# Moving one quantisation block out of the first attention, and the first feed-forward stage's start into that attention's last turn

## The reference

```python
# layer 0: attention with 32 heads of 128 (8 key/value heads), then a 4-bit linear layer
x = x + tanh(g_xattn[0]) * L0_xattn(layernorm(x), ctx, wq, wk, wv, wo)
w_fp = ((nibbles(W_q) - zero) * scale).reshape(512, 512)
x = x + tanh(g_ffn[0]) * layernorm(x) @ w_fp.T
# layer 1: attention with 32 heads of 16, then a linear layer with 28 gated low-rank experts
x = x + tanh(g_xattn[1]) * L1_xattn(rmsnorm(layernorm(x)) * ln_w, ctx)
logits = xf @ gate_W.T;  top_vals, top_idx = top_k(logits, 2);  gate = softmax(top_vals)
x = x + tanh(g_ffn[1]) * (xf @ base_W.T + lora(xf, gate))
# layer 2: attention with one head of width 512, then a SiLU layer with NF4 weights
x = x + tanh(g_xattn[2]) * softmax(Q @ K.T / sqrt(512)) @ features
normalized = w / absmax(block of 64)
dq = NF4_CODE[searchsorted(bounds, normalized)] * absmax        # for w1, w2 and w3
x = x + tanh(g_ffn[2]) * (silu(x @ dq1.T) * (x @ dq2.T)) @ dq3.T
# layer 3: attention with 32 heads of 128, then stream mixing with a Sinkhorn iteration
```

## Time and profile before

| what | value |
|---|---|
| median of three runs | 1779.58 us |
| profiled execution, its own time | 1778.58 us |
| its span in the trace | 1776.9 us |
| PE busy | 1436.3 us (81%) |
| DVE busy | 1172.7 us (66%) |
| ACT busy | 607.6 us (34%) |
| POOL busy | 357.5 us (20%) |
| TensorE clock granted in the profiled execution | 0.896 of full speed |

### The profile page before, as it was taken

One profiled execution on the slowest core, in us unless ns is written; L12 is line 12 of the kernel. 1 busy time (PEld: TensorE's weight loads), 2 busy tenths in 40 slices (PEclk: granted clock), 3 DMA queues, 4 the chain that ended last, 5 costly groups with the idle time before them and its releaser, 6 DMA issues.

```text
span 1776.9 us, 18410 instructions
## 1 busy us (share of the span) xinstructions
PE 1436.3 (81%) x6556; PEld 1012.6 (57%) x6556; DVE 1172.7 (66%) x1816; ACT 607.6 (34%) x912; POOL 357.5 (20%) x404
## 2 busy tenths in 40 slices
PE   7999999995386885888788888799999999995104
PEld 5665665552164554656466666567777777774101
DVE  4899999989746884323544445566665666576778
ACT  3655555554212332111222111344444344442003
POOL 1222222222244002001201111121122122214500
PEclk9999999998687996895699999899999999997556
DMA  4799999998710000020101121010011011000001
GB/s 185 192 217 225 219 209 219 215 194 167 176 47 11 1 1 24 1 71 1 36 18 38 45 86 48 12 60 24 36 60 60 25 36 60 1 1 1 0 0 48
DMA packets 40128, 136.35 MB, mean 77 GB/s; under 512 B 5184, under 2 KB 11200, under 8 KB 33840
## 3 DMA queue, kind: packets, MB, share of 16 engines
q0 software_dynamic: 13824, 51.91, 15.8%
q1 hardware_dynamic: 26224, 83.38, 14.1%
HBM read 72.63 MB, written 10.75 MB: 47 GB/s over the span
## 4 chain that ended last, share of the span: by engine, by line
PE 49%; DVE 20%; DMA 11%; issue 11%; DVEq 4%; ACT 3%; POOL 1%; POOLq 1%; SPq 0%
DMA AR<-AR 11%; PE PS L151 10%; PE PS L153 9%; PE PS L152 9%; DVE AR L626 4%; PE PS L841 4%; PE PS L877 3%; DVE AR L2118 2%; DVE AR L2112 2%; DVE AR L2116 2%; PE PS L863 2%; DVE X L1854 1%; PE PS L255 1%; PE PS L1982 1%; DVE AR L632 1%
## 5 line engine op out<-in xcount | busy, mean ns | idle before, releaser
L412 POOL DMA_DIRECT2D AR<-AR x96 | 97.5, 1054 | 349.0 <-DMA AR<-AR 146.3
L508 PE MATMUL PS<-R,PT 128*128 128x512 f32 x256 | 127.9, 646 | 44.1 <-DVE X L660 44.1
L153 PE MATMUL PS<-R16r 128*128 128x512 f32 (+1 forms) x312 | 123.3, 395 | 0.0
L152 PE MATMUL PS<-R16r 128*128 128x512 f32 (+1 forms) x328 | 122.6, 374 | 0.0
L483 PE MATMUL PS<-R,HT 128*128 128x256 f32 x512 | 115.9, 379 | 0.0
L508 PEld LDWEIGHTS PS<-R,PT 128*128 128x128 f32 x256 | 50.9, 206 | 108.1 <-issue 107.2
L483 PEld LDWEIGHTS PS<-R,HT 128*128 128x128 f32 x512 | 94.8, 190 | 11.6
L151 PE MATMUL PS<-R16r,HTr 128*128 128x512 f32 (+1 forms) x224 | 92.3, 412 | 6.1 <-DVE X L1234 4.6
L151 PE MATMUL PS<-HTr,R16r 128*128 128x512 f32 (+1 forms) x240 | 89.5, 373 | 3.1 <-DVE R16r L193 1.6
L152 PE MATMUL PS<-R16r,HTr 128*128 128x512 f32 (+1 forms) x224 | 87.6, 391 | 0.0
L153 PE MATMUL PS<-HTr,R16r 128*128 128x512 f32 (+1 forms) x240 | 87.2, 363 | 0.0
(11 more groups left out here) (285 smaller groups left out, 3627.9 us busy)
## 6 DMA issues: line engine op xcount, KB each, us to landing
AR<-AR POOLq DMA_DIRECT2D x96, 528.0 KB, 6.1
OR<-in_wo SPq DMA_DIRECT2D x12, 1024.0 KB, 7.7
dequantised<-AR SPq DMA_DIRECT2D x8, 1056.0 KB, 6.4
WR<-in_w0q SPq DMA_DIRECT2D x8, 1024.0 KB, 9.6
AR<-in_w3q SPq DMA_DIRECT2D x8, 1024.0 KB, 4.8
WR<-dequantised SPq DMA_DIRECT2D x22, 256.0 KB, 2.7
AR<-in_nf SPq DMA_DIRECT2D x4, 1056.0 KB, 8.0
nf_in<-in_nf SPq DMA_DIRECT2D x4, 1056.0 KB, 6.5
```

Of the source, the lines that this page charges most:

```text
L152: nc.tensor.matmul(out, ah, bl, start=False, stop=False)
L153: return nc.tensor.matmul(out, al, bh, start=False, stop=last_)
L412: nc.gpsimd.dma_start(nf_below(g)[:, part], what[:, part], accum_op=ALU.add, max_dma_last_dim=4 * N_NF // 2).then_inc(added, 16)
L508: i = nc.tensor.matmul(bank(5 + tt), PT[:, at:at + P], vo[:, pr, b, :], start=pr == 0, stop=pr == 1)
```

## The change

1. Quantisation of block 7 (`LATE`) leaves x0. Its maxima, scaling and first two `down` masks go to f1, between the norm and the wait for the logits. Ups 0 and 1 and `lowest` come after the expert weights, ups 2 to 5 and downs 2 and 3 stand between f1's sums, and ups 6 and 7 and downs 4 and 5 at the head of a2. ACT's ramps stand in f1. POOL's accumulations stand before, in and behind `pool_norm(pool, 4)`, and the join is behind the scaling of f2's first two blocks. SP stores the block after f2's first two loads, and f2's other loads wait for that store. The masks with even numbers use space in `R16`.
2. The last four turns of x0 have DVE's unpacking one turn earlier, and hold f0's low part (now on DVE) and the norm of tiles 0 to 3 with their `low` for two. PE turns tiles 0 and 1 before the last `outputs`.
3. a1's key projection runs on PE after `outputs(30)`; the value projection stays in f0, behind its third product. PE runs f0 as one product behind each tile.
4. DVE's sums of f0 are mixed with the norm's remaining steps (`dve_f0`).

```diff
...
+        def pe_norm(pe, n, work=None, given=0):
+            for t in range(given, T + 2):
+                if t < T:
+                    pe_norm_tile(pe, n, t)
+                else:
                     pe.wait_ge(lo_ready, T * (n - 1) + t - 1)
...
         def nf_mask(g, k):
+            if g == LATE and k % 2 == 0:
+                return R16[:, 4096:4096 + N_NF]
             return nf_ring(g + 1 if k % 2 else g + 2)
...
+        def nf_store(sp, g):
...
+            if g == LATE - 1:
+                sp.dma_start(KR_W, l1kr_d).then_inc(A1["kr_in"], 16)
...
+                if u == NU0 - 1:
+                    pe.wait_ge(A0["piece_sb"], PIECES0 * NG)
+                    pe_norm_tile(pe, 1, 0)
+                    pe_norm_tile(pe, 1, 1)
                 outputs(u)
+                if u == NU0 - 2:
+                    pe_a1_keys(pe)
...
-                far(g, 2 * b + 1)
+                if g < LATE:
+                    far(act, g, 2 * b + 1)
                 if u + 2 < NU0:
                     exps(u + 2)
-                far(g, 2 * b + 2)
+                if g < LATE:
+                    far(act, g, 2 * b + 2)
...
+                if u == NU0 - 2:
+                    act.wait_ge(F0["packed"], 1)
+                    act.wait_ge(A0["s_mm"], NU0)
+                    nc.scalar.copy(Oh[:], OR[:]).then_inc(F0["w_hi"], 1)
...
-            for u in range(NU0):
+            for u in range(LATE * B):
                 g, b = divmod(u, B)
-                more = g + 1 < NG
...
+                if b:
+                    dve_stats(dve, b - 1)
                 if u + 1 < NU0:
                     norm(u + 1)
-                if b == 0:
-                    down(g, 1)
-                    down(g, 0)
-                else:
-                    if b == 2:
-                        down(g, 4)
-                    up(g, 2 * b - 1)
-                    if b == 1:
-                        down(g, 2)
-                if more and b == 2:
-                    nf_reciprocal(g + 1)
                 if u + 2 < NU0:
                     shift(u + 2)
-                if 0 < b < 3:
-                    down(g, 2 * b + 1)
-                if more and b == 0:
-                    nf_max(g + 1)
-                up(g, 2 * b)
                 if b == 0:
-                    lowest(g)
-                if b == 3:
-                    up(g, 7)
-                    dve.drain().then_inc(A0["nf_used"], 1)
-                if more and b == 3:
-                    nf_normalise(g + 1)
-                if g == NG - 1 and b == 1:
                     dve_f0_nibbles(dve)
-                if g == NG - 1 and b == 2:
+                elif b == 1:
                     dve_f0_scale(dve)
+                elif b == 2:
+                    dve_f0_low(dve)
+                    norm_scaled(dve, 1, 0)
+                    norm_scaled(dve, 1, 1)
+                else:
+                    norm_scaled(dve, 1, 2)
+                    norm_low(dve, 1, 0)
+                    norm_scaled(dve, 1, 3)
+                    norm_low(dve, 1, 1)
             add(NU0 - 1)
+            dve_stats(dve, PAIRS - 1)
...
-        F0_BANKS = (5, 7, 3)
+        F0_BANKS = (7, 5, 6)
         def pe_f0(pe):
             def product(t):
                 if t == 0:
                     pe.wait_ge(F0["split"], 1)
+                if t == 1:
                     pe.wait_ge(A0["acc"], 2 * NU0)
                 if t >= 3:
                     pe.wait_ge(F0["acc"], t - 2)
...
-                if t == 1:
-                    pe_a1_keys(pe)
-            pe.wait_ge(A0["piece_sb"], PIECES0 * NG)
-            pe_norm(pe, 1, lambda t: product(t) if t < 3 else None)
-            for t in range(3, T):
-                product(t)
+                if t == 2:
+                    pe_a1_values(pe)
+            pe_norm(pe, 1, product, 2)
...
+        def dve_f0_low(dve):
+            dve.wait_ge(F0["w_hi"], 1)
+            nc.vector.tensor_tensor(Ol[:], OR[:], Oh[:].bitcast(F32), ALU.subtract).then_inc(F0["split"], 1)
...
+        def dve_f0(dve):
+            for t in range(4, T):
+                norm_low(dve, 1, t - 2)
+                norm_scaled(dve, 1, t)
+                sum_tile(dve, F0, 0, 1, F0_BANKS, t - 4)
+            norm_low(dve, 1, T - 2)
+            norm_low(dve, 1, T - 1)
+            for t in range(4, T):
+                sum_tile(dve, F0, 0, 1, F0_BANKS, t)
...
         def pool_a1(pool):
-            pool.wait_ge(A0["nf_stored"], 16 * NG)
+            pool.wait_ge(A0["nf_stored"], 16 * LATE)
...
             pe.wait_ge(A1["kr_in"], 16)
+            pe.wait_ge(A0["shifted"], NU0)
...
+            i.then_inc(A1["kr_mm"], 1)
+        def pe_a1_values(pe):
             pe.wait_ge(A1["w_in"], 16)
+            pe.wait_ge(A0["pt_ready"], NU0)
...
+        def act_a1_keys(act):
             act.wait_ge(A1["kr_mm"], 1)
...
+        def act_a1(act):
+            act.wait_ge(A1["kr_mm"], 2)
...
+            far(act, LATE, 1)
+            far(act, LATE, 2)
...
+                if t + 3 <= NUP:
+                    far(act, LATE, t + 3)
         def dve_f1(dve):
             dve_norm(dve, 3, PAIRS - 1)
+            nf_max(dve, LATE)
+            nf_reciprocal(dve, LATE)
+            nf_normalise(dve, LATE)
+            dve.drain()
+            down(dve, LATE, 1)
+            down(dve, LATE, 0)
             dve.wait_ge(F1["lg_ready"], T)
...
-            dve_sum(dve, F1, 1, 1, (2, 3, 4, 5))
+            up(dve, LATE, 0)
+            lowest(dve, LATE)
+            up(dve, LATE, 1)
+            for t in range(T):
+                sum_tile(dve, F1, 1, 1, (2, 3, 4, 5), t)
+                if t == 0:
+                    up(dve, LATE, 2)
+                    down(dve, LATE, 2)
+                elif t == 1:
+                    up(dve, LATE, 3)
+                elif t == 2:
+                    up(dve, LATE, 4)
+                    down(dve, LATE, 3)
+                elif t == 3:
+                    up(dve, LATE, 5)
...
+            up(dve, LATE, 6)
+            up(dve, LATE, 7)
+            down(dve, LATE, 4)
+            down(dve, LATE, 5)
             dve.wait_ge(A2["mhi"], 1)
...
-            sp.wait_ge(A0["nf_stored"], 16 * NG)
+            sp.wait_ge(A0["nf_stored"], 16 * LATE)
             sp.wait_ge(A2["k_mm"], 1)
             load(0, 0)
             load(1, 1)
+            nf_store(sp, LATE)
+            sp.wait_ge(A0["nf_stored"], 16 * NG)
...
-            def low_f0():
-                pool.wait_ge(F0["w_hi"], 1)
-                pool_low(Oh[:], Ol[:], OR[:]).then_inc(F0["split"], 1)
-            pool_norm(pool, 1, low_f0)
+            pool_norm(pool, 1)
             pool_a1(pool)
             pool_f1(pool)
-            pool_norm(pool, 4)
+            accumulate(pool, LATE, 1)
+            accumulate(pool, LATE, 2)
+            def third():
+                accumulate(pool, LATE, 3)
+            pool_norm(pool, 4, third)
+            accumulate(pool, LATE, 4)
+            accumulate(pool, LATE, 5)
             pool_f2(pool, (0, 1))
+            join(pool, LATE)
...
-            act.wait_ge(F0["packed"], 1)
-            act.wait_ge(A0["s_mm"], NU0)
-            nc.scalar.copy(Oh[:], OR[:]).then_inc(F0["w_hi"], 1)
-            act_norm(act, 1)
+            act_norm(act, 1, (0, 1))
+            act_a1_keys(act)
+            act_norm(act, 1, range(2, T))
             act_a1(act)
             act_f1(act)
             act_a2(act)
...
-            dve_norm(dve, 1, PAIRS - 1)
-            dve_sum(dve, F0, 0, 1, F0_BANKS)
+            dve_f0(dve)
             dve_a1(dve)
             dve_f1(dve)
...
```

291 lines of the change are left out of this document (158 added, 133 removed).

## The result

The kernel after takes 1730.23 us, the median of four runs (1728.81 to 1735.4). Its ratio to the kernel before is 0.9729, 95% interval [0.9698, 0.9759]. Measured again beside other kernels it was 0.9730 [0.9717, 0.9743]. A fourth execution of the kernel before took 1870.4 us, over 5% above the other three, and is left out as a slow one. The forecast was 1734.0, range 1722 to 1752. The profiled execution took 1730.1 us (span 1728.4); the sum of the prediction for it was 1733.1.

The account below looks back on a forecast made before the run. DVE was taken to bound the first attention's last group, with waits in the gating stage and third attention. The profiled 1778.6 less 45.5 gave 1733.1; the median being 1.0 higher, the forecast was 1734, range 1722 to 1752.

Parts of the forecast that it names:

- POOL's path into a1: Behind f0's tile 7, ACT's copies, POOL's subtraction and key spreading let a1's norm begin at 480.7, not 526.18: 45.5 us gained.
- the hand-over: End of x0: turn 29's add at 428.6, first half done 429.4, key projection from 434.4, last outputs from 443.2.
- The 5.0: Time in us taken for PE's outputs of turn 30, between 3.67 after a short wait and 5.92 after a long one.
- Group 6: First attention, without preparing block 7: scaling gives back 2.4 us, maxima and inversion nothing; bounds 2.4 and 5.3 us.
- f0: First feed-forward stage: 3.2 us per tile at full clock, ending at 474.5 where before it ended at 528.5.
- The slow-clock rival (1746): f0's products before tile 7 all run slow, so tile 7 and POOL come 11.5 us later: 1746 us; chance 14%.
- The cover: Gating stage and third attention: waits of 10.70, 27.9 and 19.27 us hide block 7's moved work; nothing taken of 33.0 us.
- The slower rival: POOL's 9.36 us hold occurs at all six accumulations and joins, stopping DVE and PE: 56 us more, 1790 us; chance 4%.
- One argument against it: On POOL's queue: a DMA that follows a DMA pays no hold.

Follow-up runs that it names:

- after_again: The kernel after, unchanged, measured again as reference of its group: 1730.31 us, 0.9730 of the kernel before.
- late_keys_norm_first: late_only with POOL's key spreadings and the first two pairs of a1's norm ahead of its subtraction for a1's weights: 1732.33 us, 0.9742 of before.
- late_only: The kernel after with f0's start as in the kernel before, block 7's quantisation still moved: 1732.22 us, 0.9749 of before.
- pairs_first: The kernel before with f0's first two norm pairs ahead of block 7's join on POOL, the low-part subtraction directly behind it: 1769.16 us, 0.9946 of before.
- start_only: The kernel after with block 7 kept in x0, f0 started early, POOL's norm pairs between accumulations, projections behind f0's second product: 1777.22 us, 0.9999 of before.

## Why the prediction was right

**The sum.** Its one term, POOL's path into a1, was 45.5 us and measured 47.06. Most of the difference lies in the hand-over. The outputs of turn 30 started at 430.20, 0.8 us later than laid out (429.4), and took 3.67 us, not 5.0, so the key projection started at 433.71 (434.4) and the last outputs at 441.93 (443.2). The 5.0 was a value between two that occur. After 1.94 us of waiting the profile of the kernel after has 3.67; after waits of 3.1 to 3.3 us five other traces have 5.37 and one, after_again, 3.67. From a1's start on the span shortens by another 1.4 us (48.5 in all), in steps that the prediction put at nothing. The stretch up to the first expert step is 2.1 us longer than before, the gating stage 1.5 shorter, and what follows `mlo` 2.0 shorter. The first and the last are scatter as far as is known: the stretch from a1's start to the first expert step took 195.3 to 197.8 us in thirteen of the fourteen traces (196.03 and 197.44 in the two of the kernel after; the fourteenth, late_keys_norm_first, has the held step), and what follows `mlo` 980.6 to 983.5. That the three nearly cancel is luck.

**Group 6.** Predicted 2.4 us from the scaling alone; the add of turn 27 starts 2.05 sooner. The maxima were worth nothing, as said: the step behind them starts at 371.19, against 370.91 before.

**f0.** Full clock for every product (1.00 from 426 to 472), and the last sum ends at 472.81 (predicted 474.5). The slow-clock rival (1746) didn't come about: from the key projection on PE hardly stood still. The short turns were not free of it: the outputs of turn 28, after 4.46 us of waiting, took 6.57 at a clock of 0.54. The rule of the Trainium skill that speed has to be earned by activity (TensorE: Matmul & The Clock Gate, "What's actually happening") agrees with these rows; by it the short turns spoke for the slow case, and there it came true, while f0's products came behind a full key projection.

**POOL's path.** The prediction had DVE and PE idle behind f0 until POOL's key spreading ends near 481, and it ended at 478.95. What it left out is that this path is the same without the early start. It argued that PE is now 6 us sooner than POOL and took the 6 us as lost. It didn't ask when a1 would start if only the block were moved: at 482.15, as late_only shows, against 482.21. So one half of the change moves a1's start by nothing, and by the times gives 3.4 ± 3.9 us. The forecast of the total came right without knowing that, and the total alone doesn't show it.

**Where the 47 us come from** is now measured apart in late_only: 33.6 us of DVE's work out of x0 (with group 6), and 10.0 of the hold behind the join, for which pairs_first alone gave 9.6 ± 2.4. What is left, some 3.5, lies inside f0: from the first norm step to the first product it takes 4.2 us instead of 7.3, where before one norm step was held for 3.98, and the first product takes 4.4 instead of 5.1.

**The cover.** The bounds on the waits held: 2.35 us left of 10.70 (predicted about 2), 8.0 in front of the sums (under 12), 12.01 of 19.27. One detail was tighter than foreseen. In front of the first sum stood 6.2 us of work in a gap of 7.8, but that gap had been measured with PE at half clock. With PE at full clock its product is ready at 695.3, and DVE's `up` 1 ends at 696.6; PE waits 1.83 us. Against before it cost nothing, because before lost more by the clock: 48.91 us from the first expert step to the last sum against 47.39. But the prediction took nothing for the cover, and beside pairs_first, where the product is fast as well, 1.2 us of it show.

**The slower rival.** It needed POOL's holds to reach someone. They are there, but 1.61, 2.37 and 4.56 us long, and nobody waits for them. One argument against it was too broad: that a DMA behind a DMA pays no hold is so for most, but in the kernel before the accumulation at 316.40 stands behind 8.32 us of "issue", and what that is stays open. POOL's timeline of the kernel after, ahead of f2's first scaling and behind the join:

```profile
763.03 0.66 POOL L1803 COPY halfmax<-absmax 128x176 f32<-128x176 f32 x1
768.25 2.04 POOL L1808 TENSOR_TENSOR WR<-WR,absmax 128x512 f32<-128x512 f32 x2 [4.56 <-issue]
...
775.17 1.78 POOL L421 DMA_DIRECT2D AR<-AR  x2 [0.64 <-issue]
```

The store followed at 782.59, and f2's third load was issued at 808.90, 46.8 us sooner than before and 26 us behind the store.

## What to carry over

Before you count an early start as a gain, follow the other engines' queues to the next stage. Where one of them is last anyway, the start is worth little until that queue is reordered; here both together were worth more than their sum. Ask of each part of a change what the kernel would take with that part alone. Work that is moved into a gap is free up to the waits that the trace shows there, and one for one beyond; measure the gap at the clock that PE will have in it.

## What the runs showed that I had not expected

**The hold behind POOL's accumulating DMAs is not one figure.** The first one between the two instructions of a norm pair is long: 9.36 us before, 8.29 in pairs_first, 8.17 in start_only. Later ones are shorter although the issue is just as recent: 5.49, 5.79 and 6.12 in start_only. Counted from the end of the last issue, these three end after 5.8 to 6.4 us. So does the one behind the subtraction in pairs_first (6.1), of which only 1.20 shows, and so do the 1.61 and 2.37 of the kernel after (5.8); its 4.56 ends after 4.9. So a long instruction put between DMA and drain takes most of the hold. The first one doesn't fit this: in the kernel after it is 4.62 us at 424.3, over 9 us behind the issue and when the join had landed more than 3 us earlier (the next load that waits for it was issued at 420.57). What else it contains stays open.

**DVE holds POOL too.** In the kernel after two 128x2 instructions of POOL start with DVE's steps on 2112 columns and take 2.43 and 2.44 us instead of 0.22. POOL's and DVE's timelines:

```profile
704.73 2.43 POOL L230 TENSOR_SCALAR veps<-mv 128x2 f32<-128x2 f32 x1 [1.74 <-DVE mv L174]
...
715.97 2.44 POOL L230 TENSOR_SCALAR veps<-mv 128x2 f32<-128x2 f32 x1 [3.75 <-DVE mv L174]
```

```profile
704.73 2.36 DVE L648 SCALAR_TENSOR_TENSOR AR<-R,AR 128x2112 f32<-128x2112 bf16 x1
...
715.97 2.36 DVE L648 SCALAR_TENSOR_TENSOR AR<-R,AR 128x2112 f32<-128x2112 bf16 x1
```

The Trainium skill (SBUF — State Buffer, "Who interferes with whom") has a rule for this: a DVE instruction with two inputs in SBUF and a GpSimd instruction that reads SBUF exclude each other for a whole instruction. These rows agree, and so does the step of two inputs in late_keys_norm_first (2.24 us). The norm steps that POOL's subtraction held (4.73 us for one, 5.20 for two) have one such input; that section of the Trainium skill counts their form among those that can use both ports, and so they fit as well.
